# Routing and normalising operations of VectorE placed between the two maxima of a half-step

## The chip, the cores and the metric

The kernel runs on one core of a Trainium2 chip. The metric is the device time of one execution in microseconds (us). Engines are named as the profile names them: PE is TensorE (PEld its weight loads), DVE is VectorE, ACT is ScalarE, POOL is GpSimd, SP is SyncE.

## What is computed

One pre-norm decoder block for 8 sequences (B) of 256 rows (N) of width 128 (D), with 16 heads of width 8. Three sublayers, each added to its input:

```python
x = x + attn(layernorm(x))          # self attention, softmax of minus a hyperbolic distance
x = x + xattn(layernorm(x), ctx)    # cross attention over 512 context rows, with a mask
x = x + ffn(layernorm(x))           # mixture of 16 experts, 4 chosen for each row

# xattn: scores = q k' / sqrt(8), masked with -1e9, softmax, times v, output projection
# ffn:   logits = -|x - keys|^2 + x rw' + rb;  topv, topi = top_k(logits, 4)
#        w = softmax(topv);  sum over the 4 of w * (w2[e] gelu(w1[e] x + b1[e]) + b2[e])
```

## The kernel before

**Stages.** The first third of the span is the self attention, the last quarter the experts' work. Between them lies the cross attention loop, and the change is all in there. It is written out by hand as one program for each engine; semaphores alone tie the engines together, and each engine does its own program strictly in order.

**The cross loop.** It runs over the batches `b` (0 to 7), and within one over 16 half-steps `hs` (in this text "steps"). In step (b, hs) the engines do this:

- PE, `scores_x` (L1197): two mask matmuls (L1208), two score matmuls of batch b (L1216), then, if there is a next batch, `maxima(b + 1, hs)` (L1182): two matmuls (L1194) of the *next* batch's scores, into the PSUM banks m0 and m1; then two more score matmuls (L1216). After these come the products with the values (`product_x`, L1232): one set of eight in most steps, none in steps 4 and 12, two in steps 5 and 13. Last is the step's item out of the list `T_LOOP` (transposes and projections into the one bank `bps`): for a full batch n3 in step 2, turn0 3, lg 4, q1 5, kv0 6, turn1 7, kv1 8, tr 9, s0 10, proj 11, k0 12, k1 13, q0 14, k2 15, s1 in step 0 of the next.
- ACT, `weights_x`: the exponential of the step's scores (L861), then copies and small functions.
- DVE, `maximum` (L1520): two operations (L1530), each the row maximum over 512 columns of one of the two banks with the mask added. They are called M0 and M1 here. After both, whatever belongs to the step: draining items, and the routing and normalising work of earlier batches.

The order around the maxima is held by these lines; `n` numbers the steps, `i` is 0 or 1. PE's matmul i of a step waits for the maximum i of the step before, since the bank is the same one:

```python
wait(pe, mx_rdy, 2 * n + i + (1 - 2 * MAX_BANKS if c == 0 else -1))   # L1193, PE
wait(dve, mx_rdy, 2 * n + i - 1)                                     # L1527, DVE
dve.wait_ge(full, count)                                             # L1529, DVE
```

**DVE's other work in a full batch (b = 2 to 6)**, with c = b - 2 for routing and c = b - 1 for the rest: `choose` in step 4 (logits, the eight largest, their indices), `chosen` in 5 (which experts as 0/1), `shift` of the maxima's first half in 7 and of the second in 15, `place` in 9 after the drain of item tr (slots of the rows), `weigh` in 10, the residual add in 11, `stats` in 12 (mean and variance), `mask_q` in 13, `refine` in 14 (one Newton step for 1/sqrt, which writes RSTD). Its small operations depend on one another; `rch`, a `Chain`, makes each wait on a semaphore for the one before it (`link` = step and wait).

**Readers of that work.** POOL's `normal_rows` (L434) waits for RSTD and writes ROW; PE's item n3 of the next batch (step 2, in the last batch step 1) transposes ROW. POOL's `send_ready` waits for `place`'s indices and `weigh`'s weights, then sends rows by indirect DMA (L725). PE's item tr waits for `chosen`'s PK (`pick_rdy`), its item s0 in step 10 for the first `shift`. ACT's `pick_weights` (step `PICK_AT`) waits for `choose`, its `inverse_root` (step `ROOT_AT`, 13) for `stats`. The last batch (b = 7) has no maxima and its own list `T_LAST`.

Of the kernel before, what the change touches and what calls it, by code (L numbers as in the profile page):

```python
# [92 lines left out]
def decoder_block(nc, a, out):  # L93
    with ExitStack() as ctx:
# [286 lines left out]
        PICK_AT, CHOSEN_AT, WEIGH_AT = at_step(6, 4), at_step(5, 4), at_step(10, 6)  # L381
        STATS_AT, ROOT_AT, REFINE_AT = at_step(12, 8), at_step(13, 9), at_step(14, 10)
# [1001 lines left out]
        def _(dve):  # L1384
# [135 lines left out]
            def maximum(c, hs):  # L1520

                h0, t = pair(hs)
                n = c * HS + hs
                if hs == 0:
                    dve.wait_ge(mb_rdy, c + 1)
                for i in range(2):
                    wait(dve, mx_rdy, 2 * n + i - 1)  # L1527
                    bank, full, count = max_bank(c, hs, i)
                    dve.wait_ge(full, count)  # L1529
                    dve.tensor_tensor_reduce(out=junk[:, i, :], in0=bank, in1=MB[:, c % 2, t, :], scale=1.0,  # L1530
                                             scalar=-3.0e38, op0=ALU.add, op1=ALU.max,
                                             accum_out=MX[:, t, h0 + i:h0 + i + 1]).then_inc(mx_rdy, 1)

            def shift(c, half):
# [5 lines left out]
                                  ALU.mult).then_inc(qmax_rdy, 1)  # L1540
                dve.wait_ge(qmax_rdy, c * 2 + half + 1)
                dve.scalar_tensor_tensor(out=QF[:, :, hs, 25], in0=MX[:, :, hs], scalar=-1.0, in1=QF[:].bitcast(F32)[:, :, hs, 24],
                                         op0=ALU.mult, op1=ALU.subtract).then_inc(q2_rdy, 1)

            rch = Chain(dve, rt_step)

            def stats(c):

                dve.wait_ge(*t_emptied("proj", c))
                for t in range(TN * c, TN * c + TN):  # L1550
                    rch.step(dve.bn_stats(bn_st[:, t, :], X[:, t, :]))
                rch.sync()
                for t in range(TN * c, TN * c + TN):
                    rch.step(dve.bn_aggr(bn_mv[:, t, :], bn_st[:, t, :]))
                rch.sync()
                dve.tensor_scalar(VE[:, :], bn_mv[:, TN * c:TN * c + TN, 1], EPS, None, ALU.add).then_inc(ve_rdy, 1)

            def refine(c):
# [4 lines left out]
                rch.link(dve.tensor_tensor(RT_[:, :], RT_[:, :], VE[:, :], ALU.mult))  # L1563
# [3 lines left out]
            def choose(c):  # L1567

                if c == 0:
# [3 lines left out]
                                  lc[:, :].unsqueeze(1).broadcast_to([P, TN, E]), ALU.add).then_inc(t_dve, 1)  # L1573
                dve.wait_ge(*t_emptied("lg", c))
                for tt in range(TN):
                    rch.step(dve.max(TOP[:, tt, :], LG[:, tt, :]))
                rch.sync()
# [354 lines left out]
```

## Time and profile before

| | |
|---|---|
| runs | 859.93, 865.53, 865.55 us |
| median | 865.53 us |
| the profiled execution | 859.28 us, of it 857.5 us from the first to the last instruction |
| busy in the span | PE 713.5 us (83%), DVE 657.5 (77%), ACT 578.5 (67%), POOL 477.1 (56%) |
| granted TensorE clock, mean | 0.789 |
| the cross loop | from about 376 to 648 us of the span |

Times in the views are microseconds from the span's first instruction. A timeline row is: start, duration, engine, line, operation, out<-in, shape, count; in brackets the idle time of the engine before it and what ended that.

### The profile page before, as it was taken

Reading aid. Unit: us, or ns where it says so; the run is one execution under the profiler, and the core shown is the slowest. Engines: PE = TensorE matmul, PEld = TensorE weight load, DVE = VectorE, ACT = ScalarE, POOL = GpSimd, SP = SyncE. Lnnn points to the kernel's source line nnn. Section 1 sums busy time; section 2 is a strip of 40 time slices with the busy share of each in tenths; the row PEclk is TensorE's granted clock in tenths of the full one; section 3 lists DMA queues with packets and bytes.
Section 4 is the critical chain, followed back from the end, with each engine's and each line's share of the span. In section 5 each row is a group of like instructions: output and inputs, shape, how many; then the busy total and the mean of one; then the engine's idle time right before and its main releaser. Section 6 shows DMA issues by size and latency. Waiting matters only on the chain.

```text
span 857.5 us, 16692 instructions
## 1 busy us (share of the span) xinstructions
PE 713.5 (83%) x5462; PEld 474.6 (55%) x5504; DVE 657.5 (77%) x1662; ACT 578.5 (67%) x747; POOL 477.1 (56%) x578
## 2 busy tenths in 40 slices
PE   3435688797898786999999999999994399999996
PEld 1124455464565553554444444444342399999994
DVE  4669999999899899788788898888745255555554
ACT  2513899999999989245666766657562267777771
POOL 2134887967966797424232634645354366566663
PEclk9855555555555555659999999999997599999999
DMA  9980000000000300051050100000015222222228
GB/s 297 336 274 0 1 1 1 1 0 1 2 1 1 75 0 1 1 157 44 24 169 19 39 25 27 15 17 23 14 33 166 75 60 82 77 79 76 79 79 270
DMA packets 56868, 56.63 MB, mean 66 GB/s; under 512 B 9712, under 2 KB 49520, under 8 KB 56656
## 3 DMA queue, kind: packets, MB, share of 16 engines
q1 hardware_dynamic: 51728, 45.14, 17.9%
q0 software_dynamic: 5056, 10.43, 3.7%
q8 instruction: 46, 0.75, 0.4%
q14 instruction: 38, 0.31, 0.1%
HBM read 25.97 MB, written 29.57 MB: 65 GB/s over the span
## 4 chain that ended last, share of the span: by engine, by line
PE 54%; DVE 24%; issue 12%; POOL 3%; DMA 3%; ACT 2%; SPq 1%; DVEq 0%; POOLq 0%; ACTq 0%
PE ops L1232 7%; PE slot L1337 6%; DVE S_FB L1467 5%; PE slot L1208 5%; DVE S_YZ L1479 4%; PE bps L1350 4%; PE slot L1216 4%; PE ops L1350 4%; PE slot L1045 4%; PE ops L1068 3%; DVE X_junk L1530 3%; DVE S_YZ L1500 3%; PE tps L1194 3%; PE bps L1082 2%; PE bps L1124 1%
## 5 line engine op out<-in xcount | busy, mean ns | idle before, releaser
L606 POOL TENSOR_TENSOR S_YZ<-S_YZ 128x512 f32<-128x512 f32 x128 | 183.0, 1463 | 56.1 <-ACT S_YZ L810 55.9
L861 ACT ACTIVATE B_W<-slot 128x1024 f32<-128x1024 f32 x128 | 131.3, 1026 | 92.5 <-PE slot L1216 92.4
L1530 DVE CUSTOM_DVE_ANT_0 X_junk<-tps,X_MB 128x512 bf16<-128x512 f32 x240 | 156.2, 688 | 31.7 <-PE tps L1194 30.9
L759 POOL DMA_INDIRECT picks<-F_ROUT,F_GOAL x94 | 103.0, 1096 | 70.9 <-DVE F_ROUT L1877 50.2
L1045 PE MATMUL slot<-S_UQT,S_UKT 32*128 32x256 f32 x256 | 84.9, 477 | 52.9 <-DVE S_YZ L1479 52.1
L1045 PEld LDWEIGHTS slot<-S_UQT,S_UKT 32*128 32x128 f32 x256 | 56.7, 298 | 83.2 <-DVE S_YZ L1479 68.7
L1467 DVE TENSOR_SCALAR S_FB<-slot 128x512 f32<-128x512 f32 x128 | 84.6, 684 | 18.5 <-PE slot L1049 18.0
L725 POOL DMA_INDIRECT rows<-B_ROW,B_IDX x64 | 62.7, 980 | 50.3 <-DVE B_ROW L1601 24.2
L1479 DVE SCALAR_TENSOR_TENSOR S_YZ<-slot,S_FB 128x512 f32<-128x512 f32 x128 | 83.5, 683 | 1.9 <-DVE S_FB L1467 0.5
L1049 PE MATMUL slot<-S_GQT,S_GKT 32*128 32x256 f32 x256 | 84.8, 447 | 0.0
L1194 PE MATMUL tps<-X_KFT,X_QFT 24*128 24x512 f32 x240 | 78.7, 519 | 3.4 <-DVE X_MX L1530 1.1
L1500 DVE SCALAR_TENSOR_TENSOR S_YZ<-S_YZ 128x1024 f32<-128x1024 f32 x50 | 78.6, 1575 | 0.0
L1232 PE MATMUL ops<-B_W,X_VX 128*9 128x256 f32 x1024 | 76.4, 385 | 0.0
L983 ACT ACTIVATE F_HB<-slot,B_B 128x256 f32<-128x256 f32 x188 | 73.6, 473 | 2.0 <-PE slot L1337 2.0
L1208 PE MATMUL slot<-B_MBT,ident_bf 128*128 128x512 bf16 x214 | 69.4, 390 | 3.9 <-DVE X_MX L1530 1.0
L1216 PE MATMUL slot<-B_QFT,X_KFT 32*128 32x256 f32 x512 | 72.1, 345 | 0.0
L1216 PEld LDWEIGHTS slot<-B_QFT,X_KFT 32*128 32x128 f32 x512 | 40.9, 185 | 56.1 <-issue 56.1
L828 ACT ACTIVATE S_YZ<-S_YZ 128x2048 f32<-128x2048 f32 x32 | 61.0, 1909 | 0.5
L1049 PEld LDWEIGHTS slot<-S_GQT,S_GKT 32*128 32x128 f32 x256 | 61.1, 299 | 0.0
L819 ACT ACTIVATE S_YZ<-S_YZ 128x2048 f32<-128x2048 f32 x32 | 60.3, 1904 | 0.2
L1068 PE MATMUL ops<-S_YZ,S_VF 128*9 128x256 f32 x512 | 56.3, 599 | 3.0 <-ACT OT L836 1.9
L1337 PE MATMUL slot<-F_xTh,F_W1h 128*128 128x256 f32 x188 | 57.5, 306 | 0.0
(300 smaller groups left out, 1595.9 us busy)
## 6 DMA issues: line engine op xcount, KB each, us to landing
rows<-S_blank SPq DMA_DIRECT2D x17, 1040.0 KB, 12.4
F_RIN<-rows SPq DMA_DIRECT2D x47, 130.0 KB, 2.1
B_W<-w1T SPq DMA_DIRECT2D x16, 256.0 KB, 4.4
F_W<-w2T SPq DMA_DIRECT2D x16, 256.0 KB, 4.9
X_CT<-ctxT SPq DMA_DIRECT2D x8, 256.0 KB, 4.7
B_W<-picks SPq DMA_DIRECT2D x8, 256.0 KB, 8.9
B_W<-picks SPq DMA_DIRECT2D x4, 384.0 KB, 5.6
picks<-F_ROUT,F_GOAL POOLq DMA_INDIRECT x94
```

What stands on the lines that cost most here:

```text
L606: g.tensor_tensor(Y[:, n % YR], Y[:, n % YR], Zr[:, n % ZR], ALU.add).then_inc(f_rdy, 1)
L861: act.activation(W[:, at:at + 2, 2 * j:2 * j + 2, :].rearrange("p h t n -> p h (t n)"), E_BANKS[k % 2][:, :, :], ACT.Exp, scale=SCALE).the ...
L1045: ins = pe.matmul(slot[n % 2][:, 0, kt * N:(kt + 1) * N], UKT[r:r + 32, p, g, kt * P:(kt + 1) * P], UQT[r:r + 32, p, g, :], start=True, st ...
L1049: ins = pe.matmul(slot[n % 2][:, 1, kt * N:(kt + 1) * N], GKT[rg:rg + 32, p, v, kt * P:(kt + 1) * P], GQT[rg:rg + 32, p, :], start=True, s ...
L1194: pe.matmul(max_bank(c, hs, i)[0], QFT[r, g, t * P:(t + 1) * P], KFT[r, c % 2, g, :], start=True, stop=True).then_inc(max_bank(c, hs, i)[1 ...
L1208: pe.matmul(E[:, i, :], ident_bf[:, :], MBT[:, p, 2 * j:2 * j + 2, :].rearrange("p t n -> p (t n)"), start=True, stop=False)
L1216: ins = pe.matmul(E[:, i, tt * N:(tt + 1) * N], KFT[r:r + 32, p, g, t * P:(t + 1) * P], QFT2[r:r + 32, g, :], start=False, stop=(tt == 1))
L1232: ins = pe.matmul(ops[32 * r:32 * r + VW, g % 2, :], VX[:, b % 2, t, h, :], W[:, h % WR, t, :], start=(t == 0), stop=(t == TM - 1))
L1337: ins = pe.matmul(slot[t % 2][:, c // 2, c % 2 * SLOTS:(c % 2 + 1) * SLOTS], w[:, t % 2, c * P:(c + 1) * P], x[:, t % 2, :], start=(w is W ...
L1467: dve.tensor_scalar(FB[:, n % FR], slot[n % 2][:, 1, :], 2.0 / DENOM_MIN, None, ALU.min).then_inc(g_rdy, 1)
L1479: dve.scalar_tensor_tensor(out=Y[:, n % YR], in0=slot[n % 2][:, 0, :], scalar=0.0, in1=FB[:, n % FR], op0=ALU.max, op1=ALU.mult).then_inc( ...
L1530: dve.tensor_tensor_reduce(out=junk[:, i, :], in0=bank, in1=MB[:, c % 2, t, :], scale=1.0, scalar=-3.0e38, op0=ALU.add, op1=ALU.max, accum ...
```

## The change

Nothing is added to or removed from what is computed. `choose`, `chosen`, `weigh`, `place`, `stats`, `refine` and `shift` are cut into pieces of one to three instructions, and `maximum` into its two halves. In the steps of batches 0 to 6 a first group of pieces is put between M0 and M1 and a second one after M1. Where a piece's input was made before an M0 or M1, the wait inside the chain is still there, but its count has long been reached. The last batch keeps whole functions, at the old steps, apart from `place`, of which only the reading of the bank stays at item tr.

| step | after M1 before | between M0 and M1 now | after M1 now |
|---|---|---|---|
| 4 | choose | | logits |
| 5 | chosen | best | ranks |
| 6 | kv0 | names | kv0 |
| 7 | shift, turn1 | equal | turn1 |
| 8 | kv1 | shift_high, picks_of | picked, kv1 |
| 9 | tr, place | shift_low | tr, place_base |
| 10 | weigh | place_pick | place_sum, weigh_sum |
| 11 | proj | place_index, weigh_inverse | weigh_rows, proj |
| 12 | stats | stats_of | stats_sum |
| 13 | mask_q | stats_eps | mask_q |
| 14 | refine | | refine_first |
| 15 | shift | refine_last | shift |

The routing pieces run for b >= 2, those of stats and refine for b >= 1, the shifts for b <= 6. `PICK_AT` goes from 6 to 7, `ROOT_AT` stays 13. The diff, cut to its core:

```diff
-        PICK_AT, CHOSEN_AT, WEIGH_AT = at_step(6, 4), at_step(5, 4), at_step(10, 6)
-        STATS_AT, ROOT_AT, REFINE_AT = at_step(12, 8), at_step(13, 9), at_step(14, 10)
+        PICK_AT, ROOT_AT = at_step(7, 4), at_step(13, 9)
...
+            def maximum_of(c, hs, i):
...
+            def place_base(c):
                 rch.link(dve.tensor_tensor(POSB[:], ...
                 dve.tensor_tensor(NEXT[:, :], ...).then_inc(t_dve, 1)
+            def place_pick(c):
+                rch.sync()
                 for tt in range(TN):
                     rch.step(dve.tensor_tensor(POSQ[:, tt], ...
...
                     if not 1 <= b <= B - 2:
                         i.then_inc(t_dve, 1)
                     else:
-                        place(b - 1)
+                        place_base(b - 1)
...
+            def pieces_first(b, hs):
+                if hs == 8:
+                    shift_high(b + 1, 0)
+                if hs == 9:
+                    shift_low(b + 1, 0)
+                if b >= 2:
+                    c = b - 2
+                    if hs == 5:
+                        best(c)
...
+            def pieces_second(b, hs):
+                if hs == 15:
+                    shift(b + 1, 1)
+                if b + 2 < B and hs == 13:
+                    mask_q(b + 2)
...
             for b in range(B):
                 here = t_loop(b)
                 for hs in range(HS):
                     if b + 1 < B:
-                        maximum(b + 1, hs)
-                        if hs in (7, 15):
-                            shift(b + 1, hs // 8)
-                    if b + 2 < B and hs == 13:
-                        mask_q(b + 2)
+                        maximum_of(b + 1, hs, 0)
+                        pieces_first(b, hs)
+                        maximum_of(b + 1, hs, 1)
+                        pieces_second(b, hs)
...
-                        elif at == hs and n == "lg":
+                        elif at == hs and n == "lg" and b == B - 1:
                             choose(c)
...
-                    if b >= 2 and hs == CHOSEN_AT[b]:
-                        chosen(b - 2)
-                    if b >= 2 and hs == WEIGH_AT[b]:
-                        weigh(b - 2)
-                    if b and hs == STATS_AT[b]:
-                        stats(b - 1)
-                    if b and hs == REFINE_AT[b]:
-                        refine(b - 1)
                     if b == B - 1:
+                        if hs == 4:
+                            chosen(B - 3)
+                        if hs == 6:
+                            place_rest(B - 3)
+                            weigh(B - 3)
+                        if hs == 8:
+                            stats(B - 2)
                         if hs == 10:
+                            refine(B - 2)
                             normal_rows(dve, B - 2)
```

## Rows read from the trace of the kernel before

**Rows 1.** Busy time by stretch: batches 3 and 6 of the loop, columns named.
```profile
core 0: us, PE busy (x) PEld busy (x) DVE busy (x) ACT busy (x) POOL busy (x), PEclk, DMA share, GB/s
...
482.70:517.10 34.40, 33.77 (x319) 16.31 (x323) 29.91 (x113) 23.05 (x32) 17.63 (x29) 1.00 0.11 32
...
586.10:618.50 32.40, 31.52 (x293) 13.63 (x297) 27.46 (x107) 21.03 (x28) 13.56 (x20) 1.00 0.06 18
```

**Rows 2.** Waits of batch 3 (482.7 to 517.1 us): us in total, times, longest.
```profile
PEld tps L1194 <- DVE X_MX L1530: 1.3, 3, 0.4
```

**Rows 3.** Timeline of batch 3, ACT: exponentials of steps 7, 8, 10, 11, 12, 13.
```profile
498.13 1.03 ACT L861 ACTIVATE B_W<-slot 128x1024 f32<-128x1024 f32 x1 [1.36 <-PE slot L1216]
500.13 1.02 ACT L861 ACTIVATE B_W<-slot 128x1024 f32<-128x1024 f32 x1 [0.97 <-PE slot L1216]
...
504.58 1.03 ACT L861 ACTIVATE B_W<-slot 128x1024 f32<-128x1024 f32 x1 [0.95 <-PE slot L1216]
...
507.40 1.02 ACT L861 ACTIVATE B_W<-slot 128x1024 f32<-128x1024 f32 x1 [1.28 <-PE slot L1216]
...
509.49 1.02 ACT L861 ACTIVATE B_W<-slot 128x1024 f32<-128x1024 f32 x1 [0.59 <-PE slot L1216]
...
511.47 1.02 ACT L861 ACTIVATE B_W<-slot 128x1024 f32<-128x1024 f32 x1 [0.48 <-PE slot L1216]
```

**Rows 4.** Timeline, steps 8 and 9: M1(8), next matmuls' weights; M0(9), M1(9), same.
```profile
500.90 0.69 DVE L1530 CUSTOM_DVE_ANT_0 X_junk<-tps,X_MB 128x512 bf16<-128x512 f32 x1
...
501.98 0.18 PEld L1194 LDWEIGHTS tps<-X_KFT,X_QFT 24*128 24x128 f32 x2
...
502.62 0.69 DVE L1530 CUSTOM_DVE_ANT_0 X_junk<-tps,X_MB 128x512 bf16<-128x512 f32 x1 [0.21 <-PE tps L1194]
...
503.23 0.69 DVE L1530 CUSTOM_DVE_ANT_0 X_junk<-tps,X_MB 128x512 bf16<-128x512 f32 x1
...
503.88 0.28 PEld L1194 LDWEIGHTS tps<-X_KFT,X_QFT 24*128 24x128 f32 x2
```

**Rows 5.** Timeline, end of `place` in step 9, M0(10), and step 11's matmuls.
```profile
504.49 0.47 DVE L1610 TENSOR_TENSOR B_POSQ<-B_EQ,B_POSB 128x64 f32<-128x64 f32 x2
...
505.43 0.69 DVE L1530 CUSTOM_DVE_ANT_0 X_junk<-tps,X_MB 128x512 bf16<-128x512 f32 x1
...
506.18 0.18 PEld L1194 LDWEIGHTS tps<-X_KFT,X_QFT 24*128 24x128 f32 x1
...
506.79 0.18 PEld L1194 LDWEIGHTS tps<-X_KFT,X_QFT 24*128 24x128 f32 x1 [0.43 <-DVE X_MX L1530]
```

**Rows 6.** Timeline, step 12: M1(12), `stats`, and step 13's second matmul.
```profile
510.11 0.69 DVE L1530 CUSTOM_DVE_ANT_0 X_junk<-tps,X_MB 128x512 bf16<-128x512 f32 x1
...
510.73 0.48 DVE L1551 BATCH_NORM_STATS2 bn_st<-X 128x6 f32<-128x128 f32 x2
...
510.86 0.18 PEld L1194 LDWEIGHTS tps<-X_KFT,X_QFT 24*128 24x128 f32 x1 [0.43 <-DVE X_MX L1530]
```

**Rows 7.** Timeline of DVE: end of `refine` and the next M0; pieces in batch 2.
```profile
446.74 0.17 DVE L1564 TENSOR_SCALAR B_RTMP<-B_RTMP 128x2 f32<-128x2 f32 x1
446.94 0.16 DVE L1565 TENSOR_TENSOR B_RSTD<-B_R,B_RTMP 128x2 f32<-128x2 f32 x1
447.06 0.69 DVE L1530 CUSTOM_DVE_ANT_0 X_junk<-tps,X_MB 128x512 bf16<-128x512 f32 x1
...
458.41 0.26 DVE L1576 MAX8 B_TOP<-B_LG 128x8 f32<-128x16 f32 x2
...
460.56 0.36 DVE L1588 TENSOR_TENSOR B_EQ<-B_iota_f,B_TOPF 128x64 f32<-128x64 f32 x2
460.95 0.43 DVE L1592 TENSOR_REDUCE B_PKF<-B_EQ 128x16 f32<-128x64 f32 x2
```

**Rows 8.** Timeline around batch 7's start: POOL's rows, and item n3 on PE.
```profile
617.77 4.14 POOL L434 TENSOR_SCALAR B_ROW<-X,bn_mv,B_RSTD 128x512 f32<-128x512 f32 x2 [2.71 <-DVE B_RSTD L1565]
...
622.06 0.41 PE L1150 MATMUL bps<-ident,B_ROW 128*128 128x128 f32 x2 [0.55 <-POOL B_ROW L434]
```

More of the change, by code:

```diff
@@ L1543, in shift, with stats_of @@
                                          op0=ALU.mult, op1=ALU.subtract).then_inc(q2_rdy, 1)
+            def shift(c, half):
+                shift_high(c, half)
+                shift_low(c, half)
             rch = Chain(dve, rt_step)
-            def stats(c):
+            def stats_of(c):
                 dve.wait_ge(*t_emptied("proj", c))
@@ L1554, in stats, with stats_eps, refine_first @@
                     rch.step(dve.bn_aggr(bn_mv[:, t, :], bn_st[:, t, :]))
+            def stats_eps(c):
                 rch.sync()
                 dve.tensor_scalar(VE[:, :], bn_mv[:, TN * c:TN * c + TN, 1], EPS, None, ALU.add).then_inc(ve_rdy, 1)
-            def refine(c):
+            def stats(c):
+                stats_of(c)
+                stats_sum(c)
+                stats_eps(c)
+            def refine_first(c):
                 dve.wait_ge(r0_rdy, c + 1)
@@ L1581, in choose, with names, equal @@
                                   ALU.subtract).then_inc(d4_rdy, 1)
+            def choose(c):
+                logits(c)
+                best(c)
+                ranks(c)
+            def names(c):
                 rch.sync()
-            def chosen(c):
-                rch.link(dve.tensor_copy(TOPF[:], TOPI[:]))
+                rch.step(dve.tensor_copy(TOPF[:], TOPI[:]))
+            def equal(c):
+                rch.sync()
                 for tt in range(TN):
@@ L1800, in _ @@
             shift(0, 1)
+            def pieces_first(b, hs):
[6 more added lines that the diff above has]
+                    if hs == 5:
+                        best(c)
+                    if hs == 6:
+                        names(c)
+                    if hs == 7:
+                        equal(c)
+                    if hs == 8:
+                        picks_of(c)
+                    if hs == 10:
+                        place_pick(c)
+                    if hs == 11:
+                        place_index(c)
+                        weigh_inverse(c)
+                if b >= 1:
+                    if hs == 12:
+                        stats_of(b - 1)
+                    if hs == 13:
+                        stats_eps(b - 1)
+                    if hs == 15:
+                        refine_last(b - 1)
+            def pieces_second(b, hs):
+                if hs == 15:
+                    shift(b + 1, 1)
+                if b + 2 < B and hs == 13:
+                    mask_q(b + 2)
+                if b >= 2:
+                    c = b - 2
+                    if hs == 4:
+                        logits(c)
+                    if hs == 5:
+                        ranks(c)
+                    if hs == 8:
+                        picked(c)
+                    if hs == 10:
+                        place_sum(c)
+                        weigh_sum(c)
+                    if hs == 11:
+                        weigh_rows(c)
+                if b >= 1:
+                    if hs == 12:
+                        stats_sum(b - 1)
+                    if hs == 14:
+                        refine_first(b - 1)
             for b in range(B):
```

70 lines of the change are left out of this document (54 added, 16 removed).

## The prediction

> **What bounds the kernel now.** I read the busy time by stretch first. In the cross loop PE works 33.8 of the 34.4 us of a full batch, at a granted clock of 1.00, and DVE 29.9 of them [rows 1]: PE has no room, DVE a little, and what counts is where PE waits for DVE. The waits of the batch give that: PE's weight load for the maxima waited for DVE's maxima three times, 1.3 us together [rows 2]. That sum counts only the engine's idle time and is less than what the steps lose, so I go on to the timeline.
>
> A step is as long as from one exponential to the next. Steps 7 and 12 take 2.00 and 1.98 us, step 10 takes 2.82 [rows 3]. In step 9 M0 starts at 502.62, M1 at 503.23 and ends 0.69 later, at 503.92; the weights of PE's next two matmuls load at 503.88 and, as the two together take 0.28 us and one 0.18, at 503.98: the second 0.06 after M1's end [rows 4]. The exponential follows that load by 0.60 (504.58) [rows 3]. This is the point to see: in an ordinary step PE reaches its second matmul just when M1 ends, so PE's pace and the chain "M0, M1, next second matmul" are equally long (0.61 + 0.69 + 0.06 + 0.60 = 1.96 us). In steps 4 and 12, which have no products, PE comes early and waits for M1 openly: the load at 510.86 is 0.06 behind M1's end at 510.80 [rows 6]. Only the steps with a kv item (6 and 8) or two product sets (5 and 13) have room: in step 8 M1 ends at 501.59 and the load comes at 501.98, 0.33 us later than it might [rows 4]; M0(8) was itself late then, and on time the room is 0.5.
>
> Work behind M1 is different. It delays M0 of the next step, and PE needs that only 0.6 us later than M1. `stats` in step 12 runs from 510.73 and costs PE nothing [rows 6]. Only `place` in step 9 is too long: M0(10) starts at 505.43, 0.85 behind the exponential; the first matmul of step 11 waits until 506.18, the second until 506.79, and step 10 grows from 2.0 to 2.82 us [rows 3, 5]. So the present order loses 0.82 us a full batch by late routing work, all in one step.
>
> **The change, part by part.** Instructions stay the same in number and kind. *Price of a piece.* The last operation of `refine` starts at 446.94, shows 0.16, and M0 starts at 447.06: without a wait behind it an operation costs its duration less about 0.05. With a chained wait behind it, one that shows 0.17 costs 0.20 (446.74 to 446.94) [rows 7]. In the pieces the waits are long met, so I take duration less 0.05. What lies between M0 and M1 is then: step 5 best 0.21, 7 equal 0.31, 8 shift_high and picks_of 0.14 + 0.38 [rows 7], 10 place_pick 0.42 [rows 5], 12 stats_of 0.43 [rows 6]; and by operations of the small kind at 0.12 to 0.14 each [rows 7], 6 names 0.12, 9 shift_low 0.14, 11 two of them 0.24, 13 stats_eps 0.12, 15 refine_last two with one chained wait, 0.32. Together 2.83 us in a full batch.
>
> The Trainium skill, "VectorE: DVE Perf Modes", section "The DRAIN you can't avoid", says that a semaphore between chained VectorE operations costs nothing extra, since the pipe is emptied anyway. Here 0.20 against 0.12 speaks against it [rows 7]; by the page each of some six exposed operations would cost 0.08 more, 0.5 us a batch.
>
> *What each insert does to PE.* It moves M1's end, so it counts fully where M1 frees PE, and not at all where there is room:
> - Step 5: choose (0.93 before) is now one logits operation, M0(5) is early, and two product sets give room: 0. The gain of no longer late M0(5) and M0(6) is 0 too, PE set those steps.
> - Step 6: room of the kv item: 0.
> - Step 7: +0.31, less 0.01 that was free: 2.00 becomes 2.30.
> - Step 8: 0.52. The longer step 7 lets M0(8) start 0.25 earlier against the exponential, and the room is 0.5: 0. DVE then does picked and kv1 (0.9) and is free just at M0(9).
> - Step 9: +0.14. place's rest is gone, so M0(10) starts on time.
> - Step 10: the 0.82 of late `place` goes; 0.42 is inserted, of which 0.08 is made up since M0(10) starts a little early: 2.82 becomes 2.33, a gain of 0.49.
> - Step 11: 0.24, but M0(11) starts 0.37 early: 0.
> - Step 12: +0.43, fully, since PE already waits there: 1.98 becomes 2.41.
> - Step 13: M0 early and two product sets: 0. Step 14: no first piece: 0.
> - Step 15: +0.32 (an ordinary step).
>
> Sum +0.31 + 0.14 - 0.49 + 0.43 + 0.32 = +0.71 us, in batches 2 to 5: +2.84. Batch 1 has no routing: steps 9, 12 and 15, +0.89. Batch 0 has only the shift: about +0.1. Batch 6 has no kv and no k items (32.4 us against 34.4 [rows 1]), so its step 8 has no room: +0.5 there, +0.43 in 12, and about -0.1 in 6: +0.85 with step 10 taken as even. Its step 15 has no next matmul.
>
> *What else moves.* RSTD is written in step 15 instead of the end of 14. POOL's rows then start about 0.6 us later against the loop. In full batches item n3 comes in step 2, long behind; but in batch 7 it comes in step 1, and there PE already waits for POOL: rows from 617.77, 4.14 us long, then n3 at 622.06 [rows 8]. So +0.6 once. POOL's indices and weights come 1 to 1.5 us later, and POOL waited 2.7 us before those rows [rows 8], which covers it; its indirect DMAs stand ahead of nothing else that is short. ACT's `inverse_root` in 13 needs stats_eps, now written 0.8 us into step 13, before its exponential of 1.02 us ends [rows 3]: 0. Item tr needs PK, now ready in step 8, one step before: 0, but the margin of three steps is down to one. The drain of kv1 ends before tr as now, s0 finds the first shift done: 0.
>
> Total: 2.84 + 0.89 + 0.1 + 0.85 + 0.6 = +5.3 us on the profiled execution of 859.3 us, 864.6. The three runs show two levels, 859.9 and twice 865.5; the profiled one lies at the lower, the median at the upper. I put the same 5.3 on the median: 870.8, rounded 870.5.
>
> **Rivals.** *A: it gains.* PE's second matmul is not held by M1 in ordinary steps; PE's own pace holds it and has a few tenths to spare, so that the inserts are hidden. Then only the late `place` goes: 0.82 in four batches and about 0.5 in batch 6, 3.8 us less, 861.7 on the median. For it: the profile names only three waits a batch [rows 2]. Against it: one of the three is step 12, where an insert costs all of its 0.43, and the load 0.06 behind M1 in step 9 [rows 4, 6]. It wins if the exposed inserts come to under 0.4 us a batch.
>
> *B: slower by over 1%.* The room that I count in steps 5, 6, 8, 11 and 13 isn't there, because inserts in a row keep DVE behind and M0 never starts early. Then all 2.83 us count, less 0.82: +2.0 in four batches, +1.2 in batch 1, +2.0 in batch 6, 0.3 in batch 0, and 0.6: 12.1 us, 877.6. It decides from 1.5 us a batch. For it: step 8, with 0.52 inserted and 0.9 behind, fills its 2.48 us step nearly. Against it: a batch's work on DVE doesn't grow, and it has 4.5 us idle [rows 1].
>
> *C: nothing.* Gains of the shorter chains (0.08 for each wait met, some ten a batch) and `place` against the inserts: within 1 us of before, 865.5.
>
> *D: the price with the wait.* If an inserted operation costs what it costs in a chain, some six exposed ones at 0.08 give +0.5 a batch, 5 x 0.5 more: 873.3. The page above would have it so.
>
> **How the numbers follow.** Forecast 0.58, A 0.18, B 0.10, C 0.08, D 0.06. The range runs from A's 861.5 to 878 above B; what lies outside is under 2 in 10. About 1% is what a measurement of this kernel can tell from no change: 8.7 us. Over it lie B, and part of D and the forecast if the two levels fall badly: slower 0.16. Faster by over 1% needs 8.7 us, twice what A gives: 0.03. Within 1%: 0.81.
>
> **What would show it.** In the timeline of a full batch of the changed kernel: step 10 at about 2.3 us and M0(10) on time (right about `place`); steps 7, 12 and 15 at 2.3, 2.4 and 2.3 us, with the second weight load of L1194's successor 0.06 us behind M1's end (right about the inserts). The waits of PE for DVE's maxima rise from three a batch to six or so and from 1.3 to over 2 us, a batch takes 35.1 us instead of 34.4, and n3 in batch 7 waits longer for POOL. If steps 7 and 15 stay at 2.0, A is right; if steps 8 and 11 grow as well, B is. A lower granted clock in the loop, or tr waiting for PK, would make it wrong in a way that I don't count.

## The result and the profile after

| | before | after |
|---|---|---|
| median of the timed runs, us | 865.37 (859.45 to 868.29, 9 runs) | 868.79 (863.75 to 872.88, 9 runs) |
| ratio of times, with 95% interval | | 1.0055 (1.0028 to 1.0081) |
| profiled execution, us | 859.3 | 867.46 |
| its span, us | 857.5 | 865.7 |
| first to last exponential of the cross loop, us | 269.92 | 273.47 |
| PE, DVE busy in the span, us | PE 713.5, DVE 657.5 | PE 719.3, DVE 651.7 |

The kernel became slower by half a per cent, which is less than the 1% named ahead as a clear difference, though the interval lies wholly above 1; forecast were 870.5 us and a loss of 5.3 us. The two profiled executions lie 8.2 us apart, and that is not what the change did: only 3.55 us of it are in the loop. The lengths of the batches, each from its first exponential to the next one's (for batch 7, to its last), say where.

| batch | 0 | 1 | 2 | 3 | 4 | 5 | 6 | 7 |
|---|---|---|---|---|---|---|---|---|
| before | 37.87 | 34.29 | 34.36 | 34.36 | 34.68 | 34.35 | 32.36 | 27.65 |
| after | 38.02 | 35.16 | 34.76 | 34.77 | 35.11 | 34.75 | 32.72 | 28.18 |
| difference | +0.15 | +0.87 | +0.40 | +0.41 | +0.43 | +0.40 | +0.36 | +0.53 |
| forecast | +0.1 | +0.89 | +0.71 | +0.71 | +0.71 | +0.71 | +0.85 | +0.6 |

In the views of the changed kernel the helpers have moved by a few lines: L860 is the exponential (L861 before), L1193 the matmuls for the maxima (L1194), L1215 the score matmuls (L1216), L1528 the maxima (L1530). First the busy time of batch 3 by stretch, which answers to [rows 1]; PE has as little room as before, at the same granted clock of 1.00.

```profile
core 0: us, PE busy (x) PEld busy (x) DVE busy (x) ACT busy (x) POOL busy (x), PEclk, DMA share, GB/s
489.20:523.95 34.75, 33.85 (x320) 16.27 (x321) 28.60 (x112) 22.95 (x31) 17.87 (x29) 1.00 0.11 32
```

The waits of batch 3 on the maxima (us in total, times, longest), against [rows 2]: there are not twice as many, as I had said, but nearly the same number, of which one is much longer.

```profile
PEld tps L1193 <- DVE X_MX L1528: 1.4, 3, 0.8
...
PE tps L1193 <- DVE X_MX L1528: 0.5, 1, 0.5
```

Now the timeline of batch 3, from step 7 to the first exponential of batch 4. The first DVE row is M1(7); a PEld row with x2 holds the weights of both maxima matmuls of the step.

```profile
503.88 1.02 ACT L860 ACTIVATE B_W<-slot 128x1024 f32<-128x1024 f32 x1 [1.46 <-PE slot L1215]
504.78 0.68 DVE L1528 CUSTOM_DVE_ANT_0 X_junk<-tps,X_MB 128x512 bf16<-128x512 f32 x1
505.24 0.46 PEld L1193 LDWEIGHTS tps<-X_KFT,X_QFT 24*128 24x128 f32 x2
506.13 1.02 ACT L860 ACTIVATE B_W<-slot 128x1024 f32<-128x1024 f32 x1 [1.13 <-PE slot L1215]
...
508.63 1.02 ACT L860 ACTIVATE B_W<-slot 128x1024 f32<-128x1024 f32 x1 [1.48 <-PE slot L1215]
...
509.25 0.30 DVE L1548 SCALAR_TENSOR_TENSOR X_QF<-X_MX,X_QF 128x16 fp32r<-128x16 f32 x1
509.48 0.68 DVE L1528 CUSTOM_DVE_ANT_0 X_junk<-tps,X_MB 128x512 bf16<-128x512 f32 x1
509.48 1.27 POOL L636 TENSOR_TENSOR X_KF<-X_KV,X_KF 128x512 fp32r<-128x512 f32 x1
...
510.81 1.02 ACT L860 ACTIVATE B_W<-slot 128x1024 f32<-128x1024 f32 x1 [1.16 <-PE slot L1215]
511.37 0.35 DVE L1683 TENSOR_TENSOR B_POSQ<-B_EQ,B_POSB 128x64 f32<-128x64 f32 x2
511.64 0.69 DVE L1528 CUSTOM_DVE_ANT_0 X_junk<-tps,X_MB 128x512 bf16<-128x512 f32 x1
512.10 0.47 PEld L1193 LDWEIGHTS tps<-X_KFT,X_QFT 24*128 24x128 f32 x2
512.99 1.02 ACT L860 ACTIVATE B_W<-slot 128x1024 f32<-128x1024 f32 x1 [0.66 <-PE slot L1215]
...
515.08 1.02 ACT L860 ACTIVATE B_W<-slot 128x1024 f32<-128x1024 f32 x1 [0.59 <-PE slot L1215]
...
516.10 0.67 DVE L1528 CUSTOM_DVE_ANT_0 X_junk<-tps,X_MB 128x512 bf16<-128x512 f32 x1
516.84 0.18 PEld L1193 LDWEIGHTS tps<-X_KFT,X_QFT 24*128 24x128 f32 x1 [0.82 <-DVE X_MX L1528]
517.43 1.03 ACT L860 ACTIVATE B_W<-slot 128x1024 f32<-128x1024 f32 x1 [0.85 <-PE slot L1215]
...
521.76 1.02 ACT L860 ACTIVATE B_W<-slot 128x1024 f32<-128x1024 f32 x1 [0.46 <-PE slot L1215]
...
523.99 1.02 ACT L860 ACTIVATE B_W<-slot 128x1024 f32<-128x1024 f32 x1 [0.71 <-PE slot L1215]
```

Read each step as the prediction does: end of M1, then the second weight load, then 0.60 us to the next exponential. Step 7: M1 starts at 504.78 and ends at 505.46; the two loads together end at 505.70, the second alone takes 0.18 and so begins at 505.52, which is 0.06 behind M1; 0.61 later is 506.13. Step 10: M1 ends at 512.33, the second load begins at 512.39, the exponential is at 512.99. Step 12: M1 ends at 516.77, load 516.84, exponential 517.43. So the chain of the prediction holds in each changed step. In steps 7 and 10 the profile shows no wait, though M1 sets the time there as much as in step 12. The weight load is only stretched, to 0.46 and 0.47 for two instead of 0.18 and 0.28 [rows 4]: where the profile shows the two loads as one row, PE's waiting lies inside it.

All steps of batch 3, in us:

| step | 0 | 1 | 2 | 3 | 4 | 5 | 6 | 7 | 8 | 9 | 10 | 11 | 12 | 13 | 14 | 15 |
|---|---|---|---|---|---|---|---|---|---|---|---|---|---|---|---|---|
| before | 2.00 | 1.93 | 2.12 | 1.88 | 1.97 | 2.36 | 2.49 | 2.00 | 2.48 | 1.97 | 2.82 | 2.09 | 1.98 | 2.36 | 1.98 | 1.93 |
| after | 1.93 | 1.98 | 2.12 | 1.82 | 1.97 | 2.36 | 2.48 | 2.25 | 2.50 | 2.18 | 2.18 | 2.09 | 2.35 | 2.36 | 1.97 | 2.24 |

Steps 7, 9, 12 and 15 give 0.25 + 0.21 + 0.37 + 0.31 = 1.14 us away, step 10 wins 0.64; the rest (0.07 and 0.06 less in steps 0 and 3, 0.05 and 0.02 more in 1 and 8) leaves +0.40. Item n3 in batch 7, against [rows 8], with POOL's rows ahead of it:

```profile
625.75 4.14 POOL L433 TENSOR_SCALAR B_ROW<-X,bn_mv,B_RSTD 128x512 f32<-128x512 f32 x2 [2.26 <-DVE B_RSTD L1590]
630.03 0.41 PE L1149 MATMUL bps<-ident,B_ROW 128*128 128x128 f32 x2 [1.09 <-POOL B_ROW L433]
```

PE waited 1.09 us for it instead of 0.55, and step 1 of batch 7 grew from 2.38 to 2.92 us.

The other 4.4 us of the difference between the spans lie ahead of the loop, where the two kernels run the same operations: the first of the maxima in the stage before it starts at 351.0 in the one and at 355.4 in the other, and stage and tail are then equally long (tail 210.76 and 210.98 us). In the rows below, from the groups by line (duration min/median/max in ns, first and last start) and from the stretch 300 to 350 us, the two kernels stand one after the other.

Before:

```profile
L1530 DVE CUSTOM_DVE_ANT_0 X_junk<-slot,X_MB x16: 680/686/692, 351.0 to 374.0; 128x512 bf16<-128x512 f32 x16
300.00:350.00 50.00, 40.26 (x260) 25.92 (x260) 44.83 (x89) 42.06 (x30) 36.70 (x29) 0.58 0.00 1
```

After:

```profile
L1528 DVE CUSTOM_DVE_ANT_0 X_junk<-slot,X_MB x16: 680/686/692, 355.4 to 378.4; 128x512 bf16<-128x512 f32 x16
300.00:350.00 50.00, 39.83 (x228) 25.95 (x232) 45.30 (x88) 41.28 (x28) 34.95 (x27) 0.53 0.00 1
```

The granted clock is the thing that differs there, 0.58 against 0.53. The gap of 4.4 us is about that between the two levels of the prediction, 859.9 and 865.5.

### The profile page after: what moved, and what is told of

Its sections match the earlier page's. It is cut to its first block, busy times and chain, and to the rows that moved or that the text cites. A ratio compares the mean times of both kernels' runs of the same rounds, so it can differ in the third digit from the quotient of the medians.

```text
span 865.7 us, 16691 instructions
## 1 busy us (share of the span) xinstructions
PE 719.3 (83%) x5462; PEld 476.8 (55%) x5504; DVE 651.7 (75%) x1662; ACT 577.8 (67%) x747; POOL 477.5 (55%) x578
## 4 chain that ended last, share of the span: by engine, by line
PE 57%; DVE 22%; issue 11%; POOL 3%; DMA 3%; ACT 2%; SPq 1%; DVEq 0%; POOLq 0%; ACTq 0%
PE ops L1231 8%; PE slot L1336 7%; DVE S_FB L1466 5%; PE slot L1207 5%; PE slot L1215 4%; DVE S_YZ L1478 4%; PE ops L1349 4%; PE bps L1349 4%; PE slot L1044 4%; PE tps L1193 3%; PE ops L1067 3%; DVE S_YZ L1499 3%; PE bps L1081 2%; DVE X_junk L1528 2%; PE bps L1123 1%
## 5 line engine op out<-in xcount | busy, mean ns | idle before, releaser
L860 ACT ACTIVATE B_W<-slot 128x1024 f32<-128x1024 f32 x128 | 131.2, 1025 | 95.7 <-PE slot L1215 95.7
L1528 DVE CUSTOM_DVE_ANT_0 X_junk<-tps,X_MB 128x512 bf16<-128x512 f32 x240 | 160.1, 687 | 44.1 <-PE tps L1193 43.0
L1193 PE MATMUL tps<-X_KFT,X_QFT 24*128 24x512 f32 x240 | 81.2, 521 | 5.5 <-DVE X_MX L1528 4.5
L1215 PE MATMUL slot<-B_QFT,X_KFT 32*128 32x256 f32 x512 | 74.1, 348 | 0.0
L1215 PEld LDWEIGHTS slot<-B_QFT,X_KFT 32*128 32x128 f32 x512 | 41.6, 185 | 55.9 <-issue 55.9
L1067 PE MATMUL ops<-S_YZ,S_VF 128*9 128x256 f32 x512 | 59.0, 623 | 3.6 <-ACT OT L835 2.5
```

Source lines behind the costliest of these rows:

```text
L860: act.activation(W[:, at:at + 2, 2 * j:2 * j + 2, :].rearrange("p h t n -> p h (t n)"), E_BANKS[k % 2][:, :, :], ACT.Exp, scale=SCALE).the ...
L1193: pe.matmul(max_bank(c, hs, i)[0], QFT[r, g, t * P:(t + 1) * P], KFT[r, c % 2, g, :], start=True, stop=True).then_inc(max_bank(c, hs, i)[1 ...
L1215: ins = pe.matmul(E[:, i, tt * N:(tt + 1) * N], KFT[r:r + 32, p, g, t * P:(t + 1) * P], QFT2[r:r + 32, g, :], start=False, stop=(tt == 1))
```

## The experiments

Three theories are to be told apart: the prediction's chain, in which an insert counts in full except where a step has room; rival A, in which ordinary steps hide it; and rival B, in which it counts everywhere. Inserted memsets write to a tile that nothing reads.

The experiments ran on four chips, which are called 2, 7, 8 and 13 here. On chip 2 the kernel before has 864.77 us, as in the timing above; on chips 8, 7 and 13 it has 902.86, 902.37 and 897.15 us. On these three DVE stands still for about 2.2 us once in nearly every batch from the second or third on, ahead of different instructions in different kernels, and the profile shows nothing that it waits for. In the experiment with the insert in step 6, for one, the waits of such a stretch name it so (us, times, longest):

```profile
DVE rec L1652 <- remote: 2.2, 1, 2.2
```

In most of these stretches TensorE idles too, and then the granted clock falls. In the kernel with the insert in step 7, TensorE idles from 497.46 to 499.64 us; the clock is 1.00 from 496 to 500 us and 0.60 from 500 to 504. Batch 3 of that kernel takes 38.30 us, where 34.36 and its insert make 34.6, so such a stop costs more than its own 2.2 us.

Batches 1 and 2 (to step 12) are free of it. The kernel before has no trace on these chips, but in the traces of three kernels with one small edit (chips 7 and 8) the steps of these batches which the edit leaves alone agree within 0.03 us with the profiled execution before. So on chips 7, 8 and 13 I read those, and trust the totals less.

### Batches' steps with an insert, ordinary and with room

A memset between M0 and M1 in one step of batches 1 to 6 of the kernel before: 288 columns (0.30 us) in step 7, the same in step 6, and 768 columns (0.70 us) in step 6.

```
                     for i in range(2):
                         ...
+                        if i == 0 and c >= 2 and hs == 7:      # 6 in the other two
+                            dve.memset(scrap[:, :], 0.0)
```

> The kernel before with one added DVE operation, a memset of 288 columns into a tile that nothing reads (0.25 to 0.3 us), between M0 and M1 of step 7 in batches 1 to 6. My theory: step 7, an ordinary step, grows by the whole of it, 2.00 to 2.27 us, and the batch from 34.36 to about 34.6. Rival (PE has room in ordinary steps): step 7 stays at 2.0.

> The same added operation between M0 and M1 of step 6 instead, the step with the item kv0, where M1 ends about 0.24 us before PE needs it. My theory: step 6 grows by 0.05 us at most (2.48 to 2.53), the batch stays at 34.4. Rival (each insert costs its whole length wherever it stands): step 6 grows by 0.27.

> The kernel before with a longer added memset, 768 columns (0.7 us), between M0 and M1 of step 6 in batches 1 to 6. My theory: the room of step 6 is about 0.24 us and what goes over it counts in full, so step 6 grows from 2.48 to 2.9 us, where the short insert cost nothing. Rival (steps with a kv item hide anything of that size): step 6 stays under 2.6.

In step 7 (chip 8): 903.87 us in one execution, against 902.86. Batch 1 of its timeline:

```profile
435.66 1.02 ACT L861 ACTIVATE B_W<-slot 128x1024 f32<-128x1024 f32 x1 [1.48 <-PE slot L1216]
436.37 0.30 DVE L1534 MEMSET X_apart<- 128x288 f32 x1
436.59 0.63 DVE L1530 CUSTOM_DVE_ANT_0 X_junk<-tps,X_MB 128x512 bf16<-128x512 f32 x1
437.02 0.43 PEld L1194 LDWEIGHTS tps<-X_KFT,X_QFT 24*128 24x128 f32 x2
437.88 1.02 ACT L861 ACTIVATE B_W<-slot 128x1024 f32<-128x1024 f32 x1 [1.20 <-PE slot L1216]
```

M1 ends at 437.22, the second load begins 0.18 before 437.45, at 437.27, and the exponential stands 0.61 behind. M0 and M1 stand 0.93 apart instead of 0.61, and M1 behind a memset shows 0.63 instead of 0.69, so M1's end moves by 0.32 - 0.06 = 0.26. Step 7 takes 2.22 to 2.23 us where it took 2.00, in batches 1, 2 and 3 alike, and step 8 another 0.03: all of the 0.26 is paid. That is the chain, and rival A is out.

In step 6 (chip 8, one execution of 895.28 us, which the stops make no measure): step 6 takes 2.51 us in batch 1, as before, and 2.48 and 2.47 in batches 2 and 3. The same insert costs nothing beside a kv item, so B is out for this step.

With 0.70 us (chip 2, 867.49 us in one execution), batch 3:

```profile
502.37 1.02 ACT L861 ACTIVATE B_W<-slot 128x1024 f32<-128x1024 f32 x1 [0.39 <-PE slot L1216]
503.43 0.70 DVE L1534 MEMSET X_apart<- 128x768 f32 x1
504.04 0.63 DVE L1530 CUSTOM_DVE_ANT_0 X_junk<-tps,X_MB 128x512 bf16<-128x512 f32 x1
504.73 0.18 PEld L1194 LDWEIGHTS tps<-X_KFT,X_QFT 24*128 24x128 f32 x1 [0.33 <-DVE X_MX L1530]
505.33 1.02 ACT L861 ACTIVATE B_W<-slot 128x1024 f32<-128x1024 f32 x1 [1.83 <-PE slot L1216]
```

M1 ends at 504.67, the load follows at 504.73 and the exponential at 505.33: step 6 takes 2.96 instead of 2.49, and PE now waits openly. M0 starts 0.25 behind the exponential, as before (502.62); M1 starts 1.42 behind M0, which with the shorter M1 moves its end by 0.81 - 0.06 = 0.75. Of these 0.47 are paid, so 0.28 us is this step's room. The kernel before says the same by the chain: M1(6) ends 1.55 us into the step, 1.55 + 0.06 + 0.60 = 2.21, and the step takes 2.49. Up to the room an insert is free, and what goes over it is paid. The room depends on when M0 starts: in batch 1 of this kernel, M0(6) starts 0.56 ahead of its exponential instead of 0.25 behind, and the same 0.70 us cost nothing (2.51 us, from 2.50). In the changed kernel the same bound shows in step 8: 1.03 us between M0 and M1 of step 8, 0.42 more than back to back, cost 0.02 there, because M0(8) came earlier in its step.

### The price of a piece in step 12

The kernel before, with the two bn_stats of step 12 between M0 and M1 in batches 1 to 6 (chip 7, one execution, 900.34 us).

```
+                    if i == 0 and early:                # c >= 2 and hs == 12
+                        stats_of(c - 2)
```

> The kernel before with one part of the change alone: the two bn_stats of batches 1 to 6 stand between M0 and M1 of step 12. My theory: step 12 grows from 1.98 to 2.36 us and nothing else changes, the full batch from 34.36 to 34.74. Rival (the wait of step 12 hides it): step 12 stays at 2.0.

```profile
440.87 1.02 ACT L861 ACTIVATE B_W<-slot 128x1024 f32<-128x1024 f32 x1 [0.57 <-PE slot L1216]
...
442.62 0.18 PEld L1194 LDWEIGHTS tps<-X_KFT,X_QFT 24*128 24x128 f32 x1 [0.81 <-DVE X_MX L1531]
443.22 1.02 ACT L861 ACTIVATE B_W<-slot 128x1024 f32<-128x1024 f32 x1 [0.85 <-PE slot L1216]
```

Step 12 takes 2.35 us, from 1.98, in batches 1 and 2, and batch 1 34.66 instead of 34.29. Alone, this one move costs what it costs in the changed kernel (2.35). The +0.37 is a single edit's price, not a sum of several.

### The last piece of `refine` back in step 14

```
-                    if hs == 15:
-                        refine_last(b - 1)
...
                     if hs == 14:
                         refine_first(b - 1)
+                        refine_last(b - 1)
```

> The changed kernel with one part undone: refine_last is back in step 14, behind M1, right after refine_first. My theory: step 15 falls from 2.24 to 1.95 us, the full batch from 34.76 to 34.5, and in the last batch step 1 (item n3 waiting for POOL's rows) from 2.92 to about 2.4 us. Rival (the wait for n3 comes from POOL's later sends, not from RSTD): step 1 of the last batch stays at 2.9.

One execution on chip 2, 865.32 us. Batch 3, the exponentials of step 15 and of the next batch, then n3 in batch 7:

```profile
521.57 1.03 ACT L860 ACTIVATE B_W<-slot 128x1024 f32<-128x1024 f32 x1 [0.48 <-PE slot L1215]
523.49 1.02 ACT L860 ACTIVATE B_W<-slot 128x1024 f32<-128x1024 f32 x1 [0.40 <-PE slot L1215]
...
624.43 4.14 POOL L433 TENSOR_SCALAR B_ROW<-X,bn_mv,B_RSTD 128x512 f32<-128x512 f32 x2 [1.73 <-DVE B_RSTD L1590]
628.72 0.41 PE L1149 MATMUL bps<-ident,B_ROW 128*128 128x128 f32 x2 [0.55 <-POOL B_ROW L433]
```

Step 15 is back at 1.93 us (2.24 in the changed kernel), n3 waits 0.55 again, and step 1 of batch 7 takes 2.38 instead of 2.92: both costs of this piece are shown. But the batch falls only by 0.21, from 34.77 to 34.56, since steps 0 and 3 go back from 1.93 and 1.82 to 1.99 and 1.88: the small gains there belonged to the later `refine_last`, and a third of its 0.31 us had come back that way. In step 0 the timeline shows how: behind the longer step 15, M0 starts 0.22 ahead of its exponential instead of 0.03 behind, and M1 no longer ends last. The loop comes to 271.93 us, 1.54 less.

### All pieces behind M1, and `place` alone

The changed kernel with the same pieces, all behind M1; and the kernel before, with the last four operations of `place` put off from step 9 to step 10, ahead of `weigh`. Both ran on chip 8.

```
                         maximum_of(b + 1, hs, 0)
-                        pieces_first(b, hs)
                         maximum_of(b + 1, hs, 1)
+                        pieces_first(b, hs)
                         pieces_second(b, hs)
```

```
                     if b >= 2 and hs == WEIGH_AT[b]:
+                        place_rest(b - 2)
                         weigh(b - 2)
```

> The changed kernel with the same pieces in the same steps, but the first group of each step moved from between M0 and M1 to behind M1. My theory (what stands between the maxima delays PE's second matmul, and that is the whole loss): steps 7, 9, 12 and 15 of a full batch go back to 2.0 us (9: up to 2.05), step 10 is 2.1 us, a full batch 33.7 to 33.8 us against 34.36 before and 34.76 changed; about 2 us less than before and 5 less than changed over the loop, ratio to before 0.997. n3 in batch 7 waits for POOL a further 0.5 us. Rival (the deferral of the pieces to later steps costs, not their place in the step): full batch stays at 34.7, ratio 1.004 to 1.006.

> The kernel before with one part of the change alone: place keeps only the two operations that read the bank in step 9, the other four go to step 10, behind M1, ahead of weigh. My theory: the late M0(10) is gone, step 10 falls from 2.82 to 1.95 us; 0.95 us of place and 0.5 of weigh then make M0(11) late, and step 11 grows from 2.09 to about 2.6, with 0.2 to 0.3 made up in step 12: full batch 33.8 us, 0.6 less than before, over five batches 3 us less, ratio 0.997. Rival (PE and not late place sets step 10): batch stays 34.3, ratio 1.000.

I had expected the first to be a little faster than the kernel before. It was slower: 909.26 us against 902.86, ratio 1.0064 (1.0031 to 1.0097). In batch 2, steps 7, 9 and 12 are at 2.00, 2.00 and 1.98, as the chain has it; step 10, which should have been near 2 us, takes 3.06, and 2.40 in batch 1, where there is no routing at all. That was a cause I did not have.

The second gave 905.27, ratio 1.0029 (0.9993 to 1.0064). Its steps came as expected: step 10 takes 1.93 instead of 2.83, while `place` and `weigh` together now make step 11 2.62 and step 12 1.55. The four steps 9 to 12 sum to 8.07 us, from 8.87. The late work had been the loss, as [rows 5] had it; but on that chip the total doesn't show the 0.8 a batch. Both were run again, on chip 7:

> The kernel with the pieces of the change in their steps but all behind M1, once more, since in its first run DVE stood still for 2.1 to 2.9 us once in each of four batches with nothing to wait for that the profile shows, and the steps around it can't be read. My theory: on a chip without such stops steps 7, 12 and 15 take 2.00, 1.97 and 1.93 us, 9 about 2.0, 10 about 2.1, a full batch 33.7 to 33.8 us; n3 in batch 7 waits 0.5 us longer than before; ratio to before 0.996 to 0.998. Rival (deferral costs): ratio over 1.002.

> The kernel before with place alone split (four of its six operations in step 10), once more for the same reason. My theory: step 10 1.95 us instead of 2.82, step 11 2.6 instead of 2.09, step 12 1.6 to 1.7 instead of 1.98: a full batch 33.7 to 33.8 us instead of 34.36, 3 us less in all, ratio 0.997. Rival: ratio 1.000 or above.

The first gave 905.17 us against 902.37, ratio 1.0021 (0.9989 to 1.0054), and the same 2.40 and 3.06; the second 905.57, 1.0018 (0.998 to 1.0056), and the same 1.93, 2.64 and 1.55. Neither ran on a chip without the stops, so what they would give there in all is not shown. The cause of the long step 10 is in the timeline of the first, here in batch 2 on chip 7:

```profile
475.62 1.28 POOL L636 TENSOR_TENSOR X_KF<-X_KV,X_KF 128x512 fp32r<-128x512 f32 x1
475.69 1.25 DVE L1548 SCALAR_TENSOR_TENSOR X_QF<-X_MX,X_QF 128x16 fp32r<-128x16 f32 x1
```

`shift_low`, 16 columns in and out, takes 1.25 us, and 0.93 in batch 1. In the kernel before all 16 of them take 0.19. Both times it ends where POOL's `tensor_tensor` ends (476.94 against 476.90, and in batch 1 442.66 against 442.61): it starts while that runs and stands until it is over. The profile books the standing as duration and not as idle time. In batch 6 of this kernel, with no such operation on POOL, it takes 0.18. The piece moved from step 8 to step 9 has met a neighbour there which step 8 does not have.

The Trainium skill, "SBUF — State Buffer", section "Who interferes with whom", says that a VectorE instruction with two SBUF inputs contends with a GpSimd instruction that reads SBUF. It also calls the shared ports an exclusive lock, and says that the order of issue decides who blocks. `shift_low` reads the maxima and QF, both in SBUF, and the trace agrees: 1.25 us against 0.19. It agrees on the two inputs too: in [rows 4] the maxima of step 9, with one input in PSUM, show their usual 0.69 us although POOL's operation begins at 503.46. By the starts that the profile shows, it does not agree on the order: in the changed kernel `shift_low` starts 0.23 us ahead of POOL's operation and is the one that grows, to 0.30, while POOL's keeps its 1.27 us.

### Shift whole in step 8

The test of that, on chip 13: the kernel with all pieces behind M1, with `shift_low` back in step 8.

```
                 if hs == 8:
-                    shift_high(b + 1, 0)
-                if hs == 9:
-                    shift_low(b + 1, 0)
+                    shift(b + 1, 0)
```

> The kernel with the pieces all behind M1, with one thing moved: the shift of the first half stands whole in step 8, instead of its second operation (shift_low, two tensor inputs in SBUF) in step 9, where it started 0.1 to 0.4 us into POOL's tensor_tensor of k_features (1.27 us) and took 0.93 to 1.25 us instead of 0.19. My theory: shift_low waits for that POOL operation; in step 8 it runs before it, takes 0.19 us again, and step 10 falls from 2.40 to 1.93 us in batch 1 and from 3.06 to about 2.1 in batch 2. Rival (shift_low is slow since it reads what the operation before the last wrote): it stays at 0.9 us or more in step 8 too and step 10 keeps its length. On a chip without the stops of DVE the ratio to before is 0.996.

894.09 us against 897.15, ratio 0.9951 (0.9914 to 0.9989), where the same kernel with `shift_low` in step 9 had been at or above the kernel before. Batch 2, `shift_low`, POOL's operation, and the exponentials of steps 10 and 11:

```profile
476.58 0.19 DVE L1548 SCALAR_TENSOR_TENSOR X_QF<-X_MX,X_QF 128x16 fp32r<-128x16 f32 x1
...
479.03 1.29 POOL L636 TENSOR_TENSOR X_KF<-X_KV,X_KF 128x512 fp32r<-128x512 f32 x1
...
479.85 1.02 ACT L860 ACTIVATE B_W<-slot 128x1024 f32<-128x1024 f32 x1 [1.21 <-PE slot L1215]
...
481.77 1.02 ACT L860 ACTIVATE B_W<-slot 128x1024 f32<-128x1024 f32 x1 [0.40 <-PE slot L1215]
```

The two no longer meet; `shift_low` takes 0.19 and step 10 takes 1.93 us (479.85 to 481.77), from 3.06. In batch 1 it is 1.92, from 2.40. Step 9 takes 2.23, since step 8 is now full. One edit took 1.13 us out of step 10, for 0.23 more in step 9, and that settles the cause. The recorded rival, that `shift_low` is slow because it reads what the operation before it wrote, is out too: in step 8 it follows that operation directly.

### The pieces behind M1, spread by room

> The changed kernel again, to have it beside the others on one chip. Both theories: about 1.005 times before, a full batch 34.76 us, steps 7, 9, 10, 12 and 15 at 2.25, 2.18, 2.18, 2.35 and 2.24 us where nothing else disturbs.

> A third arrangement of the same operations: M0 and M1 always back to back, the routing pieces behind M1 and spread so that DVE is free by the time that the next step's first matmul is done (best, ranks, names in 5; equal in 6; picks in 7; first shift in 8; place_pick, place_sum, weigh_sum in 10; index and weights in 11), stats whole in 12 and refine whole in 14 as before. My theory: no ordinary step is over 2.0 us, step 10 is 1.95, a full batch 33.5 us against 34.36 before and 34.76 changed; RSTD is as early as before, so n3 in batch 7 doesn't wait longer; 3.5 to 4 us less than before, ratio 0.995 to 0.997 on a chip that doesn't stall elsewhere. Rival (deferring routing work costs, or its gain is swallowed by PE): ratio 1.000 or above and a batch of 34.3 or more.

The second of these is the changed kernel with M0 and M1 back to back and all pieces behind M1 where a step has time: `best`, `ranks` and `names` in 5, `equal` in 6, `picks_of` and `picked` in 7, the whole shift in 8, `place_pick`, `place_sum` and `weigh_sum` in 10, `place_index`, `weigh_inverse` and `weigh_rows` in 11, `stats` in 12, `refine` in 14.

```
+            def pieces(b, hs):
                 if hs == 8:
-                    shift_high(b + 1, 0)
+                    shift(b + 1, 0)
...
                     if hs == 10:
+                        place_pick(c)
                         place_sum(c)
                         weigh_sum(c)
                     if hs == 11:
+                        place_index(c)
+                        weigh_inverse(c)
                         weigh_rows(c)
...
                         maximum_of(b + 1, hs, 0)
-                        pieces_first(b, hs)
                         maximum_of(b + 1, hs, 1)
-                        pieces_second(b, hs)
+                        pieces(b, hs)
```

Both ran on chip 2. The changed kernel again: 868.51 us (11 runs) against 864.77 (22 runs), ratio 1.0062 (1.0042 to 1.0081); its batches are within 0.01 us of those in the table above. The spread kernel: 860.32 us (12 runs), ratio 0.9956 (0.9931 to 0.998). It beats both. Its loop takes 265.87 us, 4.05 less than before and 7.6 less than the changed kernel's. A full batch takes 33.5 us; step 10 takes 1.93, step 7 2.00, step 9 1.97, step 12 1.98, step 15 1.93. Batch 3, its busy time, M0(10), and the exponentials of steps 10 and 11:

```profile
482.45:515.90 33.45, 33.23 (x325) 15.97 (x321) 29.20 (x111) 22.98 (x31) 17.78 (x29) 1.00 0.12 34
```

```profile
503.66 0.69 DVE L1528 CUSTOM_DVE_ANT_0 X_junk<-tps,X_MB 128x512 bf16<-128x512 f32 x1
503.71 1.03 ACT L860 ACTIVATE B_W<-slot 128x1024 f32<-128x1024 f32 x1 [0.94 <-PE slot L1215]
505.64 1.02 ACT L860 ACTIVATE B_W<-slot 128x1024 f32<-128x1024 f32 x1 [0.40 <-PE slot L1215]
```

M0(10) starts with its exponential instead of 0.85 behind it. PE is busy 33.23 of 33.45 us, so there is little left to win by order in a full batch. DVE's own work was never the bound; the changed kernel and this one have the same pieces, and only what stands between M0 and M1 differs, with the step that it stands in.

## Why the prediction was right, and where its terms were off

**Right in place and kind.** Time is lost in steps 7, 9, 12 and 15 and won in step 10; steps 5, 6, 8, 11 and 13 are free (in batch 3 none moved by more than 0.02, in batches 2, 4 and 5 by more than 0.03). Insert and chain are shown apart from the rest: step 7 by the memset (+0.22), step 6 by the same one (0), step 12 by `stats_of` alone (+0.37), step 15 by taking its piece out. Batch 1 came at +0.87 (said +0.89), batch 0 at +0.15 (said 0.1), n3 in batch 7 at +0.53 (said 0.6). Rival A asked for exposed inserts under 0.4 us a batch; they are 1.14. Rival B wanted steps 8 and 11 longer; they are not. Rival C, no change, lies outside both intervals and 3.55 us off in the loop. Rival D is off on the price: but for `shift_low` no piece costs more than forecast, and most cost less.

**Too large: the full batch, +0.71 said, +0.40 measured.** The terms that were off are the prices of the inserts, step 10's above all. (Step 7 stands at +0.30 in its own line and at +0.31 in the sum.)

| step | said | measured | between M0 and M1, less the 0.61 of M0 |
|---|---|---|---|
| 7 (`equal`) | +0.30 | +0.25 | 0.28, said 0.31 |
| 9 (`shift_low`) | +0.14 | +0.21 | 0.23, said 0.14 |
| 10 (`place_pick`) | -0.49 | -0.64 | 0.28, said 0.42 |
| 12 (`stats_of`) | +0.43 | +0.37 | 0.40, said 0.43 |
| 15 (`refine_last`) | +0.32 | +0.31 | 0.32, said 0.32 |

For `place_pick` I took the 0.47 us of [rows 5] as the price of its two operations. Between the maxima they show 0.35 (511.37) and displace 0.28. The difference is not one of order, but of a neighbour: in the kernel before they start at 504.49, while POOL's `tensor_tensor` runs from 503.46 for 1.27 us, to 504.73, and they read two tiles in SBUF. The groups by line (min/median/max in ns, 16 operations) show it. Before:

```profile
L1610 DVE TENSOR_TENSOR B_POSQ<-B_EQ,B_POSB x16: 210/216/336, 470.1 to 662.2; 128x64 f32<-128x64 f32 x16
```

After, where they start at 511.37 and POOL's operation had ended at 510.75:

```profile
L1683 DVE TENSOR_TENSOR B_POSQ<-B_EQ,B_POSB x16: 214/219/222, 476.6 to 670.6; 128x64 f32<-128x64 f32 x16
```

The longest took 336 ns before and 222 after. Batch 6 of the kernel before, in which POOL has no such operation, has the pair at the same place in `place` at 0.35:

```profile
606.85 0.35 DVE L1610 TENSOR_TENSOR B_POSQ<-B_EQ,B_POSB 128x64 f32<-128x64 f32 x2
```

So the wait for POOL stood inside the very row from which I priced the term, 0.12 of its 0.47. That is read from the traces; no run moved these two operations alone. POOL's small casts into QF (128x64) seem to do the same: in the spread kernel the pair in step 10 runs among them and shows 0.47 again, with 0.29 and 0.26 for its operations. It stands behind M1 there and costs nothing. In steps 7 and 12 each price was 0.03 too high. The gains of 0.07 and 0.06 in steps 0 and 3 I did not have at all.

The miss in step 9 is the same cause with the other sign: `shift_low` starts at 509.25, 0.23 ahead of POOL's `tensor_tensor`, and takes 0.30 instead of 0.19. I had listed it as one of "the small kind" without asking what POOL does then. The kernel with all pieces behind M1 shows what a start a little later costs, up to 1.06 us.

**Batch 6, +0.85 said, +0.36 measured.** Steps 8 and 12 cost 0.42 and 0.38 there, near to what was said. But I took step 10 as even, and it won 0.21; step 6 won 0.17 instead of 0.1, and step 13 0.16, with 0.17 given back in 14.

**The waits, six said, four measured.** This detail was wrong although the chain was right. In steps 7, 9 and 10 the row of the two loads is stretched (0.46, 0.49 and 0.47 us) instead of an idle time being shown. What tells is the period of the step, not the list of waits.

**The total was nearer than its worst parts.** +5.3 us was said; the loop shows +3.55, as batches 0, 1 and 7 came as said; the medians differ by 3.4 and 3.7 us, and the ratios 1.0055 and 1.0062 would be 4.8 and 5.4 us. Part of that is the level of the stage before the loop: of the runs of the kernel before 3 of 9 and 5 of 22 lie below 861 us, of the changed kernel's 20 one, 863.75, lies as far below its others. So where the ratios come nearer to 5.3 us than the loop does, that is luck and not the forecast. Of the fourteen profiled executions nine start the loop at 381.3 to 382.9 us, with a granted clock of 0.53 or 0.54 from 300 to 350 us, four at 376.8 to 376.9, with 0.58, and one, on chip 13, at 386.2 with 0.57. Whether the changed program lands more often on the upper level for a reason, or by chance, stays open; the memset kernels, whose order of work ahead of the loop is the old one, are found on both.

## What to carry to other kernels

Find the step's two chains first: here PE's pace and "M0, M1, second load" were equally long, so what stands between two maxima costs its full displacement, while what stands behind the second is free up to several tenths. Cutting late work in pieces is worth it, but put the pieces behind the operations that free the other engine's buffers, and between them only in a step whose room has been measured. And before an operation with two SBUF inputs is moved, look at what GpSimd runs at its new time.

## What the runs showed of the hardware

- A VectorE operation with two SBUF inputs that starts while GpSimd runs a `tensor_tensor` on SBUF stands until that ends: 1.25 and 0.93 us instead of 0.19, shown as its duration. Started 0.23 us before GpSimd's, it takes 0.30; a 128x64 operation, started 0.25 us before GpSimd's ends, takes 0.34 instead of 0.22. GpSimd's own operation keeps its 1.27 us each time.
- Behind a small VectorE operation of 0.16 or 0.17 us the next one starts after 0.12 us if nothing chains them and after 0.20 if a wait does [rows 7]; two unchained ones of 128x64 (0.22 us each) start 0.14 apart.
- The maxima (M) show 0.69 us and occupy 0.61 from start to start.
- The time ahead of the loop has two levels, 4.4 us apart, with a granted clock of 0.58 or 0.53 from 300 to 350 us, in 13 of 14 profiled executions; what chooses between them was not found.
- On chips 7, 8 and 13 these programs have medians of 894 to 909 us, with stops of VectorE of about 2.2 us once in most batches for which the profile shows no cause. In one of them TensorE idles for 2.18 us too, and the granted clock is 1.00 before and 0.60 in the 4 us behind; with all pieces behind M1 on chip 8, TensorE idles for 0.6 to 1.0 us in three of them and the clock stays at 1.00. Their place depends on the program. The cause is open; the totals from these chips contain the stops, and the readings by step above leave them out.
